# Cross-attention with a top-32 softmax: 22 score segments per row instead of 32, a new order of TensorE and ScalarE in a turn, queries in two buffers

## The reference, cut to what matters

```python
Q = (x_text @ Wq).reshape(Bb, Tt, H, DH)           # 4096 rows, H=4 heads of DH=32
K = (x_vision @ Wk).reshape(Bb, Gg, H, DH)         # 3202 context rows
scores = jnp.einsum('bthd,bghd->bhtg', Q, K) / np.sqrt(DH)
topv, topi = jax.lax.top_k(scores, K_TOP)          # the 32 largest of 3202, per row and head
probs = jax.nn.softmax(topv, axis=-1)
attn = jnp.zeros_like(scores).at[bi, hi, ti, topi].set(probs)
attn_mean = attn.mean(axis=1)                      # mean over the heads
V = x_vision @ Wv
c_t = jnp.einsum('btg,bgd->btd', attn_mean, V)
```

## Time and profile before

| | us |
|---|---|
| median of three runs | 4230.26 |
| profiled execution | 4228.8 |
| its span | 4227.0 |
| VectorE busy, share of the span | 3165.3, 75% |
| TensorE (PE) busy, share of the span | 3342.4, 79% |
| ScalarE (ACT) busy, share of the span | 2234.5, 53% |

### The profile page before, as it was taken

How to read it: one execution, slowest core, us unless ns; L and a number is a source line. 1 busy time by engine, 2 the same in 40 slices (tenths; PEclk the granted TensorE clock), 3 DMA queues, 4 the chain that set the end, 5 groups by cost and what they waited for, 6 DMA issues and landing times. The chain is left out here.

```text
span 4227.0 us, 54424 instructions
## 1 busy us (share of the span) xinstructions
PE 3342.4 (79%) x16624; PEld 2217.5 (52%) x16624; DVE 3165.3 (75%) x8740; ACT 2234.5 (53%) x2969; POOL 1300.7 (31%) x1174
## 2 busy tenths in 40 slices
PE   7665858888888888876967878479999999936666
PEld 3343535555555555544645555357777777712333
DVE  7699999999999999995579999334444444469996
ACT  4574858888887788883113333133333323237774
POOL 0022434444444444442020101023322332206664
PEclk9756767777777777777988999799999999968888
DMA  9600000000000000002212434534443443330111
GB/s 322 246 6 9 10 5 9 9 9 9 9 9 12 9 11 10 9 7 70 82 35 65 96 85 103 132 128 133 129 126 127 127 122 101 99 93 31 52 47 53
DMA packets 264325, 290.53 MB, mean 69 GB/s; under 512 B 55452, under 2 KB 177438, under 8 KB 263012
## 3 DMA queue, kind: packets, MB, share of 16 engines
q1 hardware_dynamic: 240728, 254.05, 19.9%
q10 hardware_dynamic: 20268, 18.34, 1.5%
q0 software_dynamic: 3040, 14.94, 0.9%
HBM read 218.82 MB, written 68.45 MB: 68 GB/s over the span
## 5 line engine op out<-in xcount | busy, mean ns | idle before, releaser
L1061 PE MATMUL score<-KT,q 64*128 64x512 f32 (+1 forms) x1792 | 670.4, 523 | 276.0 <-ACT S L918 158.1
L815 DVE MAX8 cand<-S 128x8 f32<-128x100 f32 (+1 forms) x4096 | 680.1, 245 | 69.8 <-ACT S L918 50.3
L1061 PEld LDWEIGHTS score<-KT,q 64*128 64x128 f32 x1792 | 440.4, 265 | 508.6 <-ACT S L918 220.4
L1089 PE MATMUL up<-ctx,attnT 128*128 128x384 f32 (+1 forms) x1664 | 613.4, 517 | 0.0
L918 ACT ACTIVATE S<-score 128x1024 f32<-128x1024 f32 (+1 forms) x512 | 406.5, 831 | 107.4 <-PE score L1061 107.4
L820 DVE SCALAR_TENSOR_TENSOR S<-S,tops,E 128x3202 f32<-128x3202 f32 x128 | 449.3, 3552 | 10.6 <-ACT E L949 10.6
L1089 PEld LDWEIGHTS up<-ctx,attnT 128*128 128x128 f32 (+1 forms) x1664 | 323.8, 204 | 210.3 <-issue 55.2
L2127 DVE TENSOR_TENSOR ff_gelu<-ff_whole,ff_gelu 128x512 fp32r<-128x512 f32 x128 | 98.3, 768 | 429.4 <-ACT ff_gelu L2254 429.4
L927 ACT ACTIVATE E<-S,below 128x3202 bf16<-128x3202 f32 x128 | 379.5, 2965 | 26.3 <-issue 11.9
L949 ACT ACTIVATE E<-S,ebias 128x3202 f32<-128x3202 f32 x128 | 379.7, 2967 | 1.0 <-DVE S L820 0.7
L2363 PE MATMUL ff_acc<-ff_W,ff_gelu 128*128 128x512 f32 x1024 | 345.5, 398 | 0.0
(11 more groups left out here) (361 smaller groups left out, 6017.5 us busy)
## 6 DMA issues: line engine op xcount, KB each, us to landing
s_hankel<-scratch_K SPq DMA_DIRECT2D x128, 256.0 KB, 4.4
ff_w_low<-scratch_w1l SPq DMA_DIRECT2D x112, 256.0 KB, 2.6
ff_w_low<-scratch_w2l SPq DMA_DIRECT2D x112, 256.0 KB, 2.6
xt_prep<-in_x SPq DMA_DIRECT2D x8, 1024.0 KB, 7.6
scratch_xt<-xt_prep SPq DMA_DIRECT2D x8, 1024.0 KB, 7.4
next_prep<-in_ffn_w_t POOLq DMA_DIRECT2D x8, 1024.0 KB, 11.1
q<-scratch_qt SPq DMA_DIRECT2D x128, 64.0 KB, 1.9
mod_xt<-in_x_turned SPq DMA_DIRECT2D x32, 256.0 KB, 2.7
```

Source lines behind the costliest of these rows:

```text
L815: nc.vector.max(cand[:, h, 8 * k:8 * k + 8], S[:, b, h, k * SEG:end])
L1061: last = nc.tensor.matmul(score[k % 2][:, j % 2, 0:w], lhsT=q[at, part, h // 2, :], rhs=KT[at, h // 2, chunk(j)], start=(part == 0), stop= ...
L1089: last = nc.tensor.matmul(up[:, 0:DV], lhsT=attnT[0:w, e, c - 4 * g, :], rhs=ctx[0:w, c, :], start=(c == 0), stop=(c == GC - 1))
```

## The change

Every edit is in attention, beside the constants. Shown is the core; in the rest, calls are rewritten for one group at a time, and the conditions older, old, new, newer become live(n), which is true while tile n exists or n is a loop's variable.

```diff
-SEGS = 32
-SEG = G // SEGS
+SEGS = 22
+SEG = -(-G // SEGS)
-        q = sb("q", [P, 2, H // 2, P], F32R)
+        q = sb("q", [P, 2, 2, H // 2, P], F32R)
-        FIRST = 2
+        FIRST = 3
# SyncE
-                load_queries(0)
+                load_queries(0, 0)
...
+                load_queries(1, 1)
-                with sp.Fori(0, TILES - 1) as n:
-                    sp.wait_ge(s["score_done"], GROUPS * (n + 1))
-                    load_queries(n + 1)
+                with sp.Fori(0, TILES // 2 - 1) as i:
+                    for b in range(2):
+                        sp.wait_ge(s["score_done"], GROUPS * (2 * i + b + 1))
+                        load_queries(2 * i + b + 2, b)
# VectorE: segments, exact, thresholds
-                        end = (k + 1) * SEG if k < SEGS - 1 else G
-                        nc.vector.max(cand[:, h, 8 * k:8 * k + 8], S[:, b, h, k * SEG:end])
+                        nc.vector.max(cand[:, h, 8 * k:8 * k + 8], S[:, b, h, k * SEG:min((k + 1) * SEG, G)])
...
-                        nc.vector.max(tops[:, b, h, 8 * r:8 * r + 8], src)
-                        dve.drain()
+                        if r > 0:
+                            nc.vector.max(tops[:, b, h, 8 * r:8 * r + 8], src)
+                            dve.drain()
...
-                    nc.vector.scalar_tensor_tensor(below[:, at], least, -1.0 + 2.0 ** -23, margin[:, at], ALU.mult, ALU.max).then_inc(s["below_ready"], 1)
+                    if len(heads) == 1:
+                        nc.vector.tensor_scalar(below[:, at], least, -1.0 + 2.0 ** -23, margin[:, at], ALU.mult, ALU.max).then_inc(s["below_ready"], 1)
+                    else:
+                        nc.vector.scalar_tensor_tensor(below[:, at], least, -1.0 + 2.0 ** -23, margin[:, at], ALU.mult, ALU.max).then_inc(s["below_ready"], 1)
```

More of the change, by code:

```diff
@@ L997, in turn @@
[L997 removed]
+                    if live(n - 1):
+                        probabilities(n - 1, 1 - b, 2)
+                    if live(n - 2):
                         copy_turned(n - 2, b, 3)
[L999 to L1003, removed]
[L1004 to L1006 removed]
@@ L1026, in turn @@
-                    if new:
                         count_kept(n, b, 3)
[L1028 to L1034, removed]
+                    if live(n + 1):
+                        copy_scores(n + 1, 1 - b, 1, 3)
+                        copy_scores(n + 1, 1 - b, 2, 0)
+                    if live(n - 2):
+                        copy_turned(n - 2, b, 6)
@@ L1040, in _ @@
-                turn(TILES, 0, new=False, newer=False)
-                turn(TILES + 1, 1, old=False, new=False, newer=False)
+                        turn(UNROLL * i + FIRST + j, (FIRST + j) % 2)
+                for n in range(TILES - 1, TILES + 3):
+                    turn(n, n % 2)
                 act.wait_ge(s["u_stored"], 16 * (TILES + 1))
@@ L1091, in times_context, with turn @@
                     last.then_inc(s["times_done"], 1)
[L1093 to L1098, removed]
-                        flags(n - 1)
[L1100 to L1104, removed]
+                def turn(n, b):
+                    if live(n):
+                        scores(n, b, 3, 0, "summed")
+                        scores(n, b, 3, 1, "summed")
+                    if live(n - 1):
+                        flags(n - 1)
+                    if live(n):
+                        scores(n, b, 3, 2, "summed")
+                    if live(n - 2):
+                        turn_attention(n - 2, b, 1)
+                    if live(n):
+                        scores(n, b, 3, 3, "summed")
+                    if live(n - 2):
+                        turn_attention(n - 2, b, 2)
@@ L1105, in turn @@
                         times_context(n - 2, b, 0)
[L1106 to L1109, removed]
+                        turn_attention(n - 2, b, 3)
                         times_context(n - 2, b, 1)
-                        turn_attention(n - 2, b, 4, last)
+                        turn_attention(n - 2, b, 4)
                         times_context(n - 2, b, 2)
-                    if new:
-                        scores(n, 0, range(1, 2))
@@ L1115, in turn @@
-                    if older:
-                        turn_attention(n - 2, b, 5, last)
-                        times_context(n - 2, b, 3)
[L1118 to L1124, removed]
+                    if live(n):
+                        scores(n, b, 0, 0)
@@ L1137, in _ @@
+                    if live(n - 1):
+                        turn_attention(n - 1, 1 - b, 0)
+                    if live(n + 1):
+                        scores(n + 1, 1 - b, 2, 3, "summed02")
+                    if live(n - 2):
+                        times_context(n - 2, b, 6)
+                for n in range(-1, FIRST):
+                    if n == 2:
+                        pe.wait_ge(s["ctx_in"], 32)
+                    turn(n, n % 2)
                 with pe.Fori(0, STEADY // UNROLL) as i:
@@ L1138, in _ @@
                     for j in range(UNROLL):
-                        turn(UNROLL * i + FIRST + j, j % 2)
-                turn(TILES - 2, 0)
-                turn(TILES - 1, 1, newer=False)
-                turn(TILES, 0, new=False, newer=False)
-                turn(TILES + 1, 1, old=False, new=False, newer=False, last=True)
+                        turn(UNROLL * i + FIRST + j, (FIRST + j) % 2)
+                for n in range(TILES - 1, TILES + 2):
+                    turn(n, n % 2)
 def modulate(nc, sem, const, a, W, root_table, X, dram):
```

166 lines of the change are left out of this document (94 added, 72 removed).

## The result

The changed kernel takes 4238.0 us (median of 20 runs, 4219.7 to 4248.0) against 4228.1 for the kernel before (20 runs): a ratio of 1.0019 with a 95% interval of 1.001 to 1.0028. It is slower by 10 us where 116 less was forecast, outside the range of 4052 to 4185. Its runs spread over 28 us, those of before over 7.

A forecast was written before the change was run, and what follows sets the result against it. VectorE was taken to bind at 51.09 us a turn; after the change, a ScalarE loop at 46.4. 28 intervals by 4.7, smaller gains and 35 us for a new exact call gave 117.6 less: 4112 us, range 4052 to 4185.

The forecast's parts named there:

- While VectorE binds, that costs nothing: ScalarE's spare time, 3.8 us a turn before copy_context and 2.0 before the last copy_turned, was said to cost nothing.
- the second loop: From the check over ScalarE to the next check: 41.4 + 3.0 + 1.9 = 46.3 us a turn.
- waits for scores between prob3 and the first count: ScalarE waits some 3 us a turn, as a group of scores is set behind a product of 2.75 us.
- wait for the check: ScalarE waits about 1.9 us, from head 0's count being past to VectorE being ready.
- I expect the granted clock to rise to 0.85 or more: TensorE's granted clock rises from 0.75, as TC4, TC5 and some scores fill its stretch of waits.
- case B: Rival: the order doesn't pay, ScalarE's waits only move; turn 48.0 to 50.0 us, about 4190 us; chance 0.18.
- C: Rival: TensorE's waits spread over the turn, 46% of its work at half clock; turn 53.1, about 4313 us; chance 0.05.
- the last turns: The last turn's LATE thresholds and segments were to take 2 us less.
- The exact calls: Three instead of two, the new one in tile 21 adding 35 us; each loses its first MAX8, 3.5 us.
- the queries need two buffers: With one buffer the query load would be in the open after the change; with two it costs nothing.

## Why the prediction was wrong

Two steps failed. The first made the engine that binds the wrong one; the second is the sum that gave the number.

**The wrong engine:** "So the attention runs at VectorE's pace", and with it "While VectorE binds, that costs nothing". Two runs refute it: in the old order 5.2 us less of VectorE (22 segments) and 4.7 less (23 segments) leave 51.1 and 51.2 us. The rows that spoke against it stood in the trace of before. These are ScalarE's waits there, from 600 to 1880 us:

```profile
ACT u L968 <- PE up L1089: 91.8, 25, 3.7
ACT S L918 <- PE score L1061: 67.9, 75, 1.4
ACT attnT L960 <- PE up L1089: 48.2, 25, 1.9
ACT attnT L958 <- PE up L1089: 14.4, 24, 0.8
ACT E L927 <- issue: 9.9, 47, 0.3
...
```

None is for VectorE, while VectorE waits for ScalarE's copies. By these rows the turn is ScalarE's, in step with TensorE: 41.4 us of work and 9.3 of waits, nearly all of them for TensorE, are 50.7 of the 51.1 us. I took those waits for spare time. But the rows alone don't decide, since TensorE waited 63.6 us for GpSimd behind VectorE; the run with the shorter VectorE does. That ScalarE and TensorE set the turn of before is what is left over; no run shortens ScalarE's work, and which of their waits sets it in the old order stays open.

Perfetto Trace Analysis, section "Identifying the Most-Contended Engine", in the Trainium skill calls the engine with the highest occupancy the one to improve first. By that VectorE was the engine, and I read the profile so. These runs don't agree: in the old order VectorE was at 94% in the turn, ScalarE at 81%, and 5.2 us less of VectorE moved nothing.

**The sum that failed** is the second loop, "41.4 + 3.0 + 1.9 = 46.3", from which the forecast of 46.4 came. In the 14 ordinary intervals from 651.87 to 1347.45 us the turn is 49.7, and its terms are these:

| term, us a turn | forecast | measured |
|---|---|---|
| ScalarE's work | 41.4 | 41.9 |
| waits for scores between prob3 and the first count | 3.0 | 3.2 |
| waits for scores from the first count to the sums | 0 | 2.1 (0 to 5.8) |
| wait for the check | 1.9 | 0.3 |
| before head 0's count, where the unrolled loop starts again (2.5 us, once in four turns) | 0 | 0.6 |
| other waits of ScalarE (its own queue, ebias, issue) | 0 | 1.1 |

The rest, 0.5 us, no wait names. So the largest term that was put at nothing is the stretch from the first count to the sums: the short turns have at most 0.5 us of waits for scores there, those of 51.3 to 52.5 us (but one, which has both terms) 4.8 to 5.8. The turns of 50.1 and 50.3 us have the other one:

```profile
816.18 2.96 ACT L935 ACTIVATE E<-S,below 128x3202 bf16<-128x3202 f32 x1 [2.53 <-issue]
```

This is head 0's count, the first instruction of ScalarE's turn, in every fourth turn, as the loop is unrolled four times. In the run with head 0's count earlier and no filling, where a copy of scores comes first in the turn, waits of 2.3 to 2.5 us without a releaser stand before that copy. In the traces of the old order ScalarE has no wait of this kind over 0.4 us from 600 to 1880 us.

ScalarE's waits of the changed kernel from 600 to 1880 us:

```profile
ACT S L926 <- PE score L1069: 136.4, 164, 2.4
ACT nmax L945 <- DVEq L875: 41.8, 9, 36.1
ACT E L935 <- issue: 24.1, 49, 2.6
ACT S L926 <- ACT u L976: 11.1, 16, 0.7
ACT E L957 <- POOL ebias L776: 7.8, 25, 0.3
```

The 91.8, 48.2 and 14.4 us behind products are gone, as forecast. Waits for scores doubled, 67.9 to 136.4, since a group now often stands behind a product of 2.75 us, or 5 at the half clock. (Of the 41.8 before the sums 36.1 are the exact call.) With it failed "I expect the granted clock to rise to 0.85 or more": it was 0.79 over 600 to 1880 us, from 0.75, and the lower level now lies in the stretch from counts to sums, where ScalarE waits for each group. Filling one wait shows 1.3 us a turn of it; the rest of the 3.3 between forecast and measured turn is read from the waits, not tested. That is the mechanism of the prediction's case B (waits that only move), with C's (the clock) in it. B's turn of 48.0 to 50.0 holds the measured 49.9, but its 4190 took the middle of that, and didn't count the 5.8 us of the last turns.

**What held.** 22 MAX8 over 146 take 4.75 us (4.72 said). A MAX8 over cand fell from 418 to 336 ns, the bound of head 0 from 973 to 214. VectorE's busy time fell by 5.3 us a turn (5.6 said). The exact calls: three, the third after tile 21, worth 33 to 36 us. That the queries need two buffers. **What was mis-sized besides:** the last turns were put at 2 us less and are 5.8 more.

On the clock's two rules from the Trainium skill's page TensorE: Matmul & The Clock Gate, "Loop structure matters more than you think" and "A second HAM failure mode: psum-queue depth-cycling", this case is nearer to the second for the changed kernel: with groups alternating between two score buffers and no wait of TensorE over 2.6 us in the ordinary turns from 698 to 1347 us, the grant was 0.5 in two stretches of a turn (in the long one above from 951 to 957 and from 963 to 983) and near 1 between. Filling the wait of 2.3 us raised the grant all the same, so that wait had a part in the swing, and the runs don't separate the two rules.

## What to carry to other kernels

Before calling the busiest engine the bound, ask who waits for it: list the waits of every other engine, and follow them through third engines as well. If an engine never waits for the busy one while the busy one waits for it, suspect that the loop runs through the other, however full the busy one looks, and shorten the busy one alone to find out: here that one run settled it. Waits of an engine in such a loop are not spare time, they are terms of the sum, and each stretch of the loop needs its own. When work is moved into an engine's wait, ask what then queues behind it. When data decides how often a slow path runs, count it over the inputs for every size at hand: 23 segments cost one short instruction more per head than 22 and save a call of 33 us.

## What the runs showed of the hardware

Work added to TensorE made it finish sooner: three matmuls of 2.1 us together in one wait of 2.3 us raised the granted clock from 0.81 to 0.86, and over 14 turns TensorE was busy 615.4 us instead of 623.8. In the old order eight such matmuls raised it from 0.75 to 0.85 and the time didn't move. A higher mean of the grant is thus not in itself a shorter turn; which work stands in the half-clock stretch is the likely reason, not shown by itself. A SCALAR_TENSOR_TENSOR on one column took 973 ns and on three columns 162, a TENSOR_SCALAR on one column, with the second column as a pointer, 214. The spread between runs differs too: 28 us in 20 runs of the changed kernel, 4 us in 5 runs with the wait filled, 7 us in 20 of the kernel before. The turns that fall in and out of step with the clock's swing may be why; that was not tested.
